# One shared PSUM bank for the products at a step's end, and the key exponentials moved into the next step

## What is computed

```python
q, k, v = x @ Wq.T + bq, x @ Wk.T + bk, x @ Wv.T + bv   # 16 heads of 16
q = softmax(q, axis=-1)          # over a head's 16 channels
k = softmax(k, axis=-2)          # over the batch's 1024 tokens
state = einsum('bhnd,bhne->bhde', k, v)
out = einsum('bhnd,bhde->bhne', q, state)
x = layernorm(x + layernorm(out) @ Wo.T + bo)
x = layernorm(x + cross_attention(query=x, keys_values=ctx_2048, mask))   # 8 heads, 77 keys
logits = x @ router_w
weights, index = top_k(softmax(logits), 4)
y = sum over the 4: weights * (gelu(x @ up_w[index]) @ down_w[index])
return layernorm(x + y)
```

## Time and profile before

| | us |
|---|---|
| runs | 1260.08, 1261.03, 1261.40 |
| median of the runs | 1261.03 |
| the profiled execution's own time | 1258.35 |
| its span, first to last instruction | 1256.6 |
| busy PE / DVE / ACT / POOL | 1081.1 / 741.5 / 528.1 / 642.0 |
| first up product (step 38) starts | 413.00 |
| tail starts | 621.06 |

### The profile page before, as it was taken

How to read it: one execution, slowest core, us unless ns; L and a number is a source line. 1 busy time by engine, 2 the same in 40 slices (tenths; PEclk the granted TensorE clock), 3 DMA queues, 4 the chain that set the end, 5 groups by cost and what they waited for, 6 DMA issues and landing times.

```text
span 1256.6 us, 27281 instructions
## 1 busy us (share of the span) xinstructions
PE 1081.1 (86%) x8576; PEld 910.0 (72%) x8576; DVE 741.5 (59%) x1813; ACT 528.1 (42%) x1148; POOL 642.0 (51%) x739
## 2 busy tenths in 40 slices
PE   6658887797865889989989999999999999999960
PEld 3346665575654778778878888888888888888750
DVE  2578878876984667566674444444444444444326
ACT  2766556553542355454423333333333333333214
POOL 3013322655766557676786655555555555554324
PEclk9789889887877899899999999999999999999985
DMA  5453222112111333233345644456554444553436
GB/s 142 147 161 104 79 76 78 50 31 84 38 59 34 79 57 69 56 66 73 49 80 71 91 77 77 77 77 77 77 78 77 77 77 77 77 77 61 65 47 250
DMA packets 159970, 100.63 MB, mean 80 GB/s; under 512 B 106957, under 2 KB 151169, under 8 KB 159841
## 3 DMA queue, kind: packets, MB, share of 16 engines
q1 hardware_dynamic: 129824, 63.21, 20.5%
q0 software_dynamic: 30016, 35.68, 19.4%
HBM read 49.55 MB, written 31.59 MB: 65 GB/s over the span
## 4 chain that ended last, share of the span: by engine, by line
PE 66%; DVE 14%; ACT 7%; issue 4%; DMA 4%; POOL 3%; SPq 1%; DVEq 0%; ACTq 0%; POOLq 0%
PE big L1730 28%; PE big L1749 14%; PE trans L1749 11%; PE big L1767 2%; POOL slot_records L813 2%; PE big L1673 2%; DMA w_down<-in_L_ffn_down_w_dram 1%; PE trans L1592 1%; ACT pr L954 1%; PE small L1684 1%; PE small L1652 1%; DVE w_down L1088 1%; DVE stat L1092 1%; DVE xm L1391 1%; PE trans L1662 1%
## 5 line engine op out<-in xcount | busy, mean ns | idle before, releaser
L1730 PE MATMUL big<-xgT,w_up 128*128 128x256 f16 (+1 forms) x3456 | 412.1, 269 | 10.6 <-ACT h L938 5.8
L938 ACT ACTIVATE h<-big,up_scale 128x512 f32<-128x512 f32 x270 | 185.5, 687 | 440.1 <-PE big L1730 434.9
L1730 PEld LDWEIGHTS big<-xgT,w_up 128*128 x3456 | 326.8, 99 | 55.5 <-issue 14.2
L843 POOL DMA_INDIRECT token_sums<-y,rec x135 | 222.6, 1649 | 249.7 <-ACT y L946 217.7
L1363 DVE TENSOR_SCALAR hh<-h,h_scale 128x512 f16<-128x512 f32 x270 | 132.6, 491 | 347.3 <-ACT h L938 347.0
L1749 PE MATMUL big<-w_down,hh 128*128 x1296 | 221.0, 273 | 0.8 <-DVE hl L1365 0.5
L1365 DVE SCALAR_TENSOR_TENSOR hl<-h,h_scale,hh 128x512 f16<-128x512 f32 x270 | 204.3, 757 | 9.6
L1749 PE MATMUL big<-w_down,hl 128*128 x648 | 176.7, 273 | 0.0
L828 POOL DMA_INDIRECT xg<-token_rows,rec x135 | 137.8, 1021 | 48.8 <-issue 39.3
L789 POOL TENSOR_SCALAR ve<-mv 128x1 f32<-128x1 f32 x96 | 27.1, 282 | 243.9 <-DVE mv L1096 243.4
L813 POOL DMA_INDIRECT slot_records<-recs,posi x128 | 132.4, 1034 | 34.9 <-issue 34.9
(11 more groups left out here) (261 smaller groups left out, 1413.4 us busy)
## 6 DMA issues: line engine op xcount, KB each, us to landing
w_down<-in_L_ffn_up_w_dram SPq DMA_DIRECT2D x8, 1024.0 KB, 5.1
w_down<-in_L_ffn_down_w_dram SPq DMA_DIRECT2D x7, 1024.0 KB, 5.8
wqkv_XA<-in_x_dram SPq DMA_DIRECT2D x32, 128.0 KB, 2.6
XRES<-in_x_dram SPq DMA_DIRECT2D x32, 128.0 KB, 2.3
token_sums<-X SPq DMA_DIRECT2D x32, 128.0 KB, 1.7
token_rows<-XR SPq DMA_DIRECT2D x32, 128.0 KB, 1.7
sums<-token_sums SPq DMA_DIRECT2D x8, 512.0 KB, 6.5
out_dram<-sums SPq DMA_DIRECT2D x8, 512.0 KB, 2.6
```

Of the source, the lines that this page charges most:

```text
L843: pool.indirect_dma_start(acc[0:EARLY_BATCHES * N, :] if t < EARLY else acc, bass.IndirectOffsetOnAxis(ap=rec[:, t % RING, j, 0:1], axis=0 ...
L938: act.activation(h[:, i % H_RING, :], psu[up_bank(i)], ACT.Gelu_apprx_tanh, scale=k["up_scale"][:, t:t + 1]).then_inc(gelu_ready, 1)
L1730: ins = pe.matmul(psu[up_bank(i)][:, j * size(t):(j + 1) * size(t)], w[:, ws, c, m:m + P], xgT[:, t % 2, xs * CC + c, 0:size(t)], start=(n ...
```

## The change

Five edits:

1. What a step's end produces goes to one use of a bank, "end": the values' product at columns 0 to 263, and behind it the router logits, the running counts, the early counts and the two halves of the turned context keys. `end_products(s)` issues them in a row, after one wait, and signals `end_ready` once. The bank is free when DVE has taken all of them (`small_emptied`), for which each kind has a counter of its own.
2. The two "st" products share one bank as well. DVE waits for both and then takes both.
3. DVE lowers the keys (`lower_keys`) after it has normalised X1, and no longer right after it has built the shift.
4. ACT takes the exponentials of the keys in the step after the closing step, between the copy of the turned input and the copies of the projections.
5. In the mixed steps the router logits move to "end", and with them everything that follows from them by one step: the tables CHOOSE, COUNTED, PLACED and SENT for the late halves, one more mixed step (14), and 21 early tiles.

```diff
@@ -73,13 +73,13 @@
-    {(0, 0): 21, (0, 1): 25, (1, 0): 29, (1, 1): 33, (2, 0): 38, (2, 1): 41, (3, 0): 46, (3, 1): 50})
-SENT = [list(range(23, 31)), [31, 32, 33, 34, 35, 35, 36, 36], list(range(40, 48)), [48, 48, 49, 49]]
+    {(0, 0): 21, (0, 1): 25, (1, 0): 29, (1, 1): 33, (2, 0): 38, (2, 1): 42, (3, 0): 47, (3, 1): 51})
+SENT = [list(range(23, 31)), [31, 32, 33, 34, 35, 35, 36, 36], list(range(40, 48)), [49, 49, 50, 50]]
-EARLY = 20
+EARLY = 21
...
+ROUTE0 = XH * (XD + 1)
+PLACE0 = ROUTE0 + EXP
+COUNTS0 = PLACE0 + EXP * HT
+KEYS0 = COUNTS0 + EXP
+assert KEYS0 + CC * KEYS <= 512
...
+def keys_turned(s):
+
+    b, i = divmod(s - TB - 2, TB + 1)
+    return b if i == 0 and 0 <= b < B else None
...
+def ends(s):
+
+    return (chain_tile(s, 3) is not None or chain_tile(s, 5) is not None or at_step(PLACED, s)
+            or s == COUNT_STEP or keys_turned(s) is not None)
...
-        if s >= MIX0 and c5 is not None:
-            use(sm, "rt", c5)
...
-        if c3 is not None:
-            use(sm, "pv", c3)
+        if ends(s):
+            use(sm, "end", s)
...
-            use(sm, "rt", c5)
         if state_built(s) is not None:
-            for c in range(CC):
-                use(sm, "st", state_built(s), c)
-        for b, half in at_step(PLACED, s):
-            use(sm, "pos", b, half)
-        if s == COUNT_STEP:
-            use(sm, "early")
-        b, i = divmod(s - TB - 2, TB + 1)
-        if i == 0 and 0 <= b < B:
-            for c in range(CC):
-                use(sm, "kt", b, c)
+            use(sm, "st", state_built(s))
     use(sm, "cnt")
     return tr, sm, big
 
 
 TR, SM, BIG = bank_uses()
...
+SM_ORDER = list(SM)
+END_COUNT = {key[1]: n + 1 for n, key in enumerate(key for key in SM_ORDER if key[0] == "end")}
+SM_COUNT = {key: n + 1 for n, key in enumerate(key for key in SM_ORDER if key[0] != "end")}
...
+        def route_sums(g):
+            return sm_bank(("end", route_step_of(g)))[:, ROUTE0:ROUTE0 + EXP]
+
+        def place_sums(b, half):
+            return sm_bank(("end", PLACED[b, half]))[:, PLACE0:PLACE0 + EXP * HT]
+
+        def turned_keys(b, c):
+            return sm_bank(("end", (TB + 1) * b + TB + 2))[:, KEYS0 + c * KEYS:KEYS0 + (c + 1) * KEYS]
+
+        def state_sums(b, c):
+            return sm_bank(("st", b))[:, c * (P + 1):(c + 1) * (P + 1)]
+
+        early_total = sm_bank(("end", COUNT_STEP))[:, COUNTS0:COUNTS0 + EXP]
 
         def staging(n):
...
                     copy_turned(xT, "x", after)
+                b = state_built(s)
+                if b is not None:
+                    for q in range(len(KEY_GROUPS)):
+                        act.wait_ge(ks_ready, len(KEY_GROUPS) * b + q + 1)
+                        act.activation(key_group(b, q), key_group(b, q), ACT.Exp).then_inc(ke_ready, 1)
                 if a is not None:
...
-                b = closing(s)
-                if b is not None:
-                    for q in range(len(KEY_GROUPS)):
-                        act.wait_ge(ks_ready, len(KEY_GROUPS) * b + q + 1)
-                        act.activation(key_group(b, q), key_group(b, q), ACT.Exp).then_inc(ke_ready, 1)
...
+
+            def lower_keys(b):
                 dve.wait_ge(kdown_ready, b + 1)
                 for q, (i0, i1) in enumerate(KEY_GROUPS):
                     dve.tensor_tensor(key_group(b, q), key_group(b, q), kmx[:, :].unsqueeze(1).to_broadcast([P, i1 - i0, C]), ALU.subtract
                                       ).then_inc(ks_ready, 1)
 
 ...
+                dve.wait_ge(sm_ready, SM_COUNT["st", b])
                 for c in range(CC):
-                    sp_ = small_wait(("st", b, c))
+                    sp_ = state_sums(b, c)
                     dve.reciprocal(rst[:, c:c + 1], sp_[:, P:P + 1]).then_inc(rst_ready, 1)
                     dve.wait_ge(rst_ready, CC * b + c + 1)
                     dve.scalar_tensor_tensor(out=sums_v[:, c, :], in0=sp_[:, 0:P], scalar=rst[:, c:c + 1],
-                                             in1=bias[:, 2 * C + c * P:2 * C + (c + 1) * P], op0=ALU.mult, op1=ALU.add).then_inc(sm_free, 1)
+                                             in1=bias[:, 2 * C + c * P:2 * C + (c + 1) * P], op0=ALU.mult, op1=ALU.add).then_inc(sm_free if c == CC - 1 else st_step, 1)
                 for c in range(CC):
-                    dve.wait_ge(sm_free, SM["st", b, c] + 1)
+                    dve.wait_ge(sm_free, SM_COUNT["st", b])
+                    dve.wait_ge(st_step, b + 1)
                     dve.tensor_tensor(state[:, c, 0:P].rearrange("p (h d) -> p h d", h=HPC), sums_v[:, c, :].rearrange("p (h d) -> p h d", h=HPC),
                                       bsel[:, :].unsqueeze(2).to_broadcast([P, HPC, LD]), ALU.mult).then_inc(state_ready, 1)
 
...
-                if s <= MIX0 and chain_tile(s, 6) is not None:
+                if chain_tile(s, 6) is not None:
...
+                if close is not None:
+                    lower_keys(close)
...
-                if c5 is not None:
-                    router_logits(c5)
...
+            def small_emptied(key):
+                if key[0] != "end":
+                    pe.wait_ge(sm_free, SM_COUNT[key])
+                    return
+                s = key[1]
+                if chain_tile(s, 3) is not None:
+                    pe.wait_ge(values_taken, chain_tile(s, 3) + 1)
+                if chain_tile(s, 5) is not None:
+                    pe.wait_ge(rt_taken, chain_tile(s, 5) + 1)
+                for b, half in at_step(PLACED, s):
+                    pe.wait_ge(pos_taken, HALVES * b + half + 1)
+                if s == COUNT_STEP:
+                    pe.wait_ge(early_taken, 1)
+                if keys_turned(s) is not None:
+                    pe.wait_ge(kt_taken, CC * (keys_turned(s) + 1))
+
             def small_into(key):
-                pe.wait_ge(sm_free, SM[key] - 1)
+                if SM[key] >= 2:
+                    small_emptied(SM_ORDER[SM[key] - 2])
...
+            def end_products(s):
+                if not ends(s):
+                    return
+                small_into(("end", s))
+                c3, c5, keys = chain_tile(s, 3), chain_tile(s, 5), keys_turned(s)
+                if c3 is not None:
+                    ins = context_values(c3)
+                if c5 is not None:
+                    ins = route(c5)
                 for b, half in at_step(PLACED, s):
                     pe.wait_ge(counted_ready, HALVES * b + half + 1)
-                    dst = small_into(("pos", b, half))[:, 0:EXP * HT]
-                    pe.matmul(dst, before[:, :], counted[:, :, 1:HT + 1], start=True, stop=False)
-                    pe.matmul(dst, ones[:, :], cum[:, :, 0:HT], start=False, stop=True).then_inc(sm_ready, 1)
+                    pe.matmul(place_sums(b, half), before[:, :], counted[:, :, 1:HT + 1], start=True, stop=False)
+                    ins = pe.matmul(place_sums(b, half), ones[:, :], cum[:, :, 0:HT], start=False, stop=True)
+                if s == COUNT_STEP:
+                    pe.wait_ge(counted_ready, HALVES * EARLY_BATCHES)
+                    ins = pe.matmul(early_total, ones[:, :], counted[:, :, 0], start=True, stop=True)
+                if keys is not None:
+                    pe.wait_ge(ctx_loaded, 16 * (keys + 1))
+                    for c in range(CC):
+                        ins = pe.transpose(turned_keys(keys, c), ctx_sb[:, c * P:(c + 1) * P], ident[0:KEYS, 0:KEYS])
+                ins.then_inc(end_ready, 1)
...
                 if c5 is not None:
                     turn_second(c5)
-                if c3 is not None:
-                    context_values(c3)
-                if c5 is not None:
-                    route(c5)
+                end_products(s)
                 last = state_built(s)
                 if last is not None:
                     pe.wait_ge(kv_ready, 2 * TB * (last + 1))
                     if last == 0:
                         pe.wait_ge(consts, CONST_STEPS)
                     for c in range(CC):
-                        dst = small_into(("st", last, c))
+                        if c == 0:
...
-                        ins.then_inc(sm_ready, 1)
-                positions(s)
-                if s == COUNT_STEP:
-                    pe.wait_ge(counted_ready, HALVES * EARLY_BATCHES)
-                    pe.matmul(small_into(("early",))[:, 0:EXP], ones[:, :], counted[:, :, 0], start=True, stop=True).then_inc(sm_ready, 1)
-                b, i = divmod(s - TB - 2, TB + 1)
-                if i == 0 and 0 <= b < B:
-                    pe.wait_ge(ctx_loaded, 16 * (b + 1))
-                    for c in range(CC):
-                        pe.transpose(small_into(("kt", b, c))[:, 0:KEYS], ctx_sb[:, c * P:(c + 1) * P], ident[0:KEYS, 0:KEYS]).then_inc(sm_ready, 1)
+                    ins.then_inc(sm_ready, 1)
 
```

97 lines of the change are left out of this document (52 added, 45 removed), and 4 rows, old and new, of the table PARTED.

## The result

The changed kernel takes 1241.41 us (median of 4 runs, 1238.87 to 1246.55), the kernel before 1260.55 (median of 4). The ratio is 0.9853, with a 95% interval of 0.9820 to 0.9886. The forecast was 1242.5, so its sign and its size came out. The profiled execution took 1240.24 us with a span of 1238.5, against 1239.9 worked out for it. The sum fits; its terms are right only in part, and effects of the clock that it left out nearly cancelled each other in this execution.

The account below looks back on a forecast made before the run. Ahead of the tail, DVE and PE wait for each other in turn, so DVE's idle times were counted. Gains less losses of 1.1 and 1.3 sum to 18.5 us, from 1261.0 to 1242.5; range 1231 to 1256.

Parts of the forecast that it names:

- Turned keys: Steps 19 and 28: DVE's waits for keys and projections go once PE turns keys behind the logits; 3.7 and 3.8 us.
- Running counts: Steps 25 and 29: DVE's waits for the counts and the heads or projections behind them shrink; 2.0 and 4.2 us.
- a clock that stays low: Step 29: if PE stays at the slow clock, projections take twice as long and only about 2.2 of 4.6 us remain.
- Closing step and state: Steps 17 to 19 and 26 to 28: four changes together gain 2.0 us for batch 1 and 2.0 for batch 2.
- some 2 us earlier: Closing step and state: PE starts the state products directly behind the logits, some 2 us earlier, as ACT and PE are ahead.
- No loss: Step 18: ACT's copy of the projected keys begins at about 161.9, against 161.87 before, despite the exponentials ahead of it.
- First batch: Steps 8 and 9: exponentials ahead of ACT's copy of the projected keys cost DVE 1.1 us; bounds 0 and 2.3.
- Start of the mixed steps: First up product at 409.5 to 410 instead of 413.00, needing only its rows and ACT's bank; gain 3.2 us, bounds 1 and 4.
- Mixed steps: One more mixed step loses 0.6 us and counts ahead of the last up product 0.7; together 1.3 lost, bounds 0 and 4.
- Handed on: Rival, chance 0.16: stalls go but ACT and POOL take their place; only 6.0 us gained, 1255.
- More than that: Rival, chance 0.13: PE keeps full clock from 148 on and 0.8 us projection waits go; some 12 us more, 1230.
- Slower: Rival, chance 0.08: in the mixed steps the bank returns too late for "wo"; 21 us lost, net 1263.5.

Follow-up runs that it names:

- second profile: The changed kernel itself, with no edit, timed and profiled once more beside the kernel before: 1243.02 us, ratio 0.9867.

## Why the prediction was right

**Turned keys: right.** 3.7 and 3.8 us were expected, 3.9 and 4.0 measured (tiles 17 to 18 and 25 to 26), and undoing this alone brings the stalls back. Of each 3.9, some 1.6 us are the projections, which run in 1.88 us once the stall ahead of them is gone and took 3.51 behind it. That DVE's waits are to be counted and not PE's 4.13 us is not shown by the size: 3.9 lies between the two.

**Running counts: right, and incomplete.** The waits of 1.1 us for the counts are gone. For step 25, tiles 23 to 24 took 25.34 us before and 25.17 and 23.96 after, at clocks of 0.84, 0.81 and 0.86, and 25.87 with the counts apart at 0.87: 1.4 to 1.9 us at like clocks, for 2.0. Step 29 gave 3.3 us in one profile and 5.0 in the other for 4.2; the difference is 1.68 us, about what the projections lose when they run at the lower clock (1.88 to 3.5 us). In three experiments (the bank alone, and two with filling) tiles 26 to 27 took 11.56 to 11.60 us at 0.70 or 0.71, a gain of 1.6 to 1.7: the prediction's case of a clock that stays low, for which it gave 2.2. Step 33 was left out of the sum. DVE's waits of 0.71 us for the counts and 1.41 for the projections stood there too, of which 1.15 remain, and the stretch became 1.9 us shorter.

**Closing step and state: too large, and wrong in the reason.** 2.0 us were expected for batch 1 and 1.5 measured (44.33 to 42.85), but step 15, which lost no stall, gives 1.5 by its clock alone. The rest, tiles 15 to 17, took 33.30 us before and 33.36 and 33.22 after, each of these with more low clock than before; two experiments with the exponentials in the next step, at the clocks of the kernel before (0.92 and 1.00), took 32.28 and 32.31. So the term is about 1.0 us, and 2.0 with the bank alone (31.31). The step that failed is "some 2 us earlier" for the state products. They began 5.10 us after DVE's take of tile 16 before and 4.97 and 4.99 after, since PE waits 1.1 us for ACT's copy of the turned shares, which now stands behind the exponentials; with the bank alone it is 3.91. "No loss" for the copy of the keys failed beside it: it began at 161.61, near the 161.9 worked out, but DVE was ready 1.52 us ahead of it, not 0.45. That was one of the prediction's own signs of being wrong, over 1 us of DVE ahead of this copy, and it came in steps 9 (1.32 us) and 18, not in 27. For batch 2 state and counts together gave 2.9 and 0.8 us for 4.0; step 27 alone (tiles 24 to 25) took 12.32 us before and 9.60 and 12.88 after, at clocks of 0.91, 1.00 and 0.73, so the clock moves it by more than the term.

**First batch: right in sign.** -1.1 and -0.8 for -1.1, and DVE's wait for the copy (1.32 and 0.98 us) is there and goes with the exponentials behind the copies. The match in size is not firm, as the stretch is -0.7 with the bank alone too.

**Start of the mixed steps: the size is not settled.** 3.2 us were taken, 1.2 and 1.5 measured from the last scatter on in the two profiles. The bank that ACT leaves was taken for the last condition; the rows' arrival (2.92 us of waiting at 400.71) came later. It was named as the lower bound. Two experiments that leave this part and the scatters alone, exponentials behind the copies and counts apart, took 17.37 and 17.14 us there, a gain of 2.8 and 3.1, near the value taken.

**Mixed steps: sign wrong, size small.** Set against steps of one kind, 13 mixed steps take 201.42 us; those of before take 206.79 less three times 1.65, or 201.8. Nor does the extra step show: from the 53rd to the 69th gelu, which holds it, it is 48.93 us before and 48.40 and 46.75 after. The 5.4 us that the first profile gains in the 13 steps are clock.

**The clock: what the sum left out.** In the profiled execution it took 4.2 us between tiles 19 and 20, 1.7 between 27 and 30 and 1.6 in step 18, and gave 5 us in the mixed steps and 1.5 in step 15. These nearly cancel, and so the total fitted: that the forecast and the measured time differ by only 1 us is luck. In the second profile the mixed steps were 1.3 us longer than before, not 5.4 shorter, and the kernel was 2.8 us slower than in the first. By the Trainium skill ("TensorE: Matmul & The Clock Gate", section "What's actually happening") activity releases the throttle; the filled mixed steps agree, at a clock of 1.00 for 0.96, though the first profile of the changed kernel had 1.00 there without filling. The inference drawn ahead of the result, that fewer stalls give clock back elsewhere, was not borne out between tiles 19 and 20.

**The rivals.** "Handed on" described much of what the state term did, not the whole. "More than that" asked for the full clock from 148 us on; from 148 to 390 it was 0.89, for 0.86 before. "Slower" asked for idle PE ahead of `wo` in the mixed steps: from 409 us to the tail the changed kernel's trace shows none over 0.3 us there.

## What to carry to other kernels

Where two engines hand small results to and fro through two buffers, each product that is third in a row waits for a whole step of the other engine; put products that are read together into one buffer, and reckon the gain by the reader's waits. Work moved to where an engine is idle on average can still stand ahead of copies that other engines wait for. Behind the first such copy it still held up the second here, so place it behind the last of them, or where no engine waits. Where PE has a gap in each step of a stage that it otherwise bounds, matmuls that nobody reads, no longer than the gap, cost nothing and may keep its clock up: here they were worth 6.8 of 208 us in the profiles and 7.9 us in the medians.
